# A decoder layer's attention scores recast as float32r products of high and low parts

## What is computed

```python
scores = jnp.einsum('bqhd,bkhd->bhqk', q, k) / sqrt(16)       # self
attn = jax.nn.softmax(scores, axis=-1)
...
scores = jnp.einsum('bhqd,bhkd->bhqk', q, k) / sqrt(16)       # cross
scores = jnp.where(mask == 0, jnp.float32(-1000000000.0), scores)
attn = jax.nn.softmax(scores, axis=-1)
```

## Time and profile before

| what | us |
|---|---|
| median of 3 runs | 2195.06 (2192.9 to 2195.93) |
| the profiled execution: its span, first to last instruction | 2190.0 |
| PE busy | 2124.8 |
| DVE busy | 1197.9 |
| ACT busy | 991.8 |
| POOL busy | 652.9 |

### The profile page before, as it was taken

How to read it: one execution, slowest core, us unless ns; L and a number is a source line. 1 busy time by engine, 2 the same in 40 slices (tenths; PEclk the granted TensorE clock), 3 DMA queues, 4 the chain that set the end, 5 groups by cost and what they waited for, 6 DMA issues and landing times. The chain is left out here.

```text
span 2190.0 us, 48112 instructions
## 1 busy us (share of the span) xinstructions
PE 2124.8 (97%) x18818; PEld 1490.5 (68%) x18818; DVE 1197.9 (55%) x2512; ACT 991.8 (45%) x1514; POOL 652.9 (30%) x1011
## 2 busy tenths in 40 slices
PE   8999999999999999999999999998799999999996
PEld 4566666666666666666666666665567877778785
DVE  4657667767667777667767766765311111111146
ACT  2445555555555555555555555555322222222233
POOL 2212332333332333332323332332421212122244
PEclk8999999999999999999999999999799999999998
DMA  3331112111111001101000100000023224331363
GB/s 98 100 104 50 36 42 74 34 50 57 34 33 33 28 27 34 32 24 29 24 24 31 33 26 27 24 25 16 21 59 80 50 53 90 80 75 30 85 214 154
DMA packets 96285, 116.98 MB, mean 53 GB/s; under 512 B 11360, under 2 KB 89005, under 8 KB 94016
## 3 DMA queue, kind: packets, MB, share of 16 engines
q1 hardware_dynamic: 66640, 82.37, 11.7%
q0 software_dynamic: 17184, 19.66, 5.0%
q10 hardware_dynamic: 12240, 11.88, 1.6%
HBM read 65.84 MB, written 56.05 MB: 56 GB/s over the span
## 5 line engine op out<-in xcount | busy, mean ns | idle before, releaser
L913 DVE TENSOR_REDUCE smax<-ps_s 128x4 f32<-128x1024 f32 x508 | 619.9, 1220 | 311.7 <-PE ps_s L614 277.2
L798 ACT ACTIVATE prob<-ps_e 128x1024 f32<-128x1024 f32 x508 | 519.7, 1023 | 499.9 <-PE ps_e L623 407.8
L614 PE MATMUL ps_s<-stack 17*128 17x256 f32 x4064 | 581.0, 403 | 20.1 <-DVE smax L913 13.6
L623 PE MATMUL ps_e<-stack 18*128 18x256 f32 x4064 | 580.1, 403 | 0.5 <-ACT prob L798 0.5
L614 PEld LDWEIGHTS ps_s<-stack 17*128 17x128 f32 x4064 | 353.4, 186 | 201.3 <-issue 103.6
L623 PEld LDWEIGHTS ps_e<-stack 18*128 18x128 f32 x4064 | 350.0, 186 | 1.5 <-DMA stack<-nrows 0.7
L1706 ACT ACTIVATE hid<-m_ps_h,b_sb 128x320 f32<-128x320 f32 x256 | 134.6, 527 | 392.3 <-PE m_ps_h L1660 392.3
L1660 PE MATMUL m_ps_h<-m_cols,w_sb 128*128 128x320 f32 x1024 | 290.8, 433 | 0.6 <-DVE m_cols L1729 0.6
L1677 PE MATMUL m_ps_o<-w_sb,hid 128*128 128x256 f32 x1280 | 279.2, 380 | 1.3 <-DVE m_res L1758 1.3
L1677 PEld LDWEIGHTS m_ps_o<-w_sb,hid 128*128 128x128 f32 x1280 | 243.8, 190 | 35.8 <-DVE m_res L1758 1.7
L639 PE MATMUL ps_w<-prob,val 128*32 128x256 f32 x4096 | 250.5, 386 | 1.2 <-ACT prob L798 1.2
(11 more groups left out here) (145 smaller groups left out, 2233.3 us busy)
## 6 DMA issues: line engine op xcount, KB each, us to landing
w_sb<-in_w SPq DMA_DIRECT2D x16, 1024.0 KB, 6.4
slot_rows_dram<-w_sb ACTq DMA_DIRECT2D x40, 258.0 KB, 2.6
m_rows<-slot_rows_dram SPq DMA_DIRECT2D x15, 645.0 KB, 4.4
xT<-in_xT SPq DMA_DIRECT2D x32, 256.0 KB, 2.9
ctxT<-in_ctxT SPq DMA_DIRECT2D x32, 256.0 KB, 2.9
x_res<-in_x SPq DMA_DIRECT2D x32, 256.0 KB, 2.8
sums_dram<-x SPq DMA_DIRECT2D x32, 256.0 KB, 2.1
c_rows<-sums_dram SPq DMA_DIRECT2D x8, 1024.0 KB, 15.9
```

Of the source, the lines that this page charges most:

```text
L614: mm = nc.tensor.matmul(scores[:, p % 2, t, :], rows_of_s[rows, Q, p // HG, t * P:(t + 1) * P], rows_of_s[rows, K, p // HG, :], start=True ...
L623: mm = nc.tensor.matmul(shifted[:, p % 2, t, :], rows_of_e[rows, K, h // HG, t * P:(t + 1) * P], rows_of_e[rows, Q, h // HG, :], start=Tru ...
L798: nc.scalar.activation(prob[:, h:h + 2, :].rearrange("p h s -> p (h s)"), shifted[:, :, :, :].rearrange("p h t s -> p (h t s)"), ACT.Exp, ...
L913: nc.vector.tensor_reduce(max_columns(X, p), scores[:, :, :, :], AX.X, ALU.max)\
```

## The change

Queries and keys are split into a high part that float32r holds exactly and the remainder, so that products of parts can be made in float32r matmuls that add up in PSUM.

- `padded` loses its mask and maximum rows. A strip of 32 now holds for keys the 16 features twice, for queries the 16 high and the 16 low parts. `stack` becomes three float32r tiles: `stack_q` (high and low queries), `stack_kh` (ACT's rounding copy of the keys) and `stack_kl` (the remainder, by DVE's new `key_remainders`, PSUM minus `stack_kh`). 
- A score is `stack_q` times `stack_kh` plus `stack_q` times `stack_kl`, 32 rows each. Mask and maxima stand in separate tiles `aux_q`, `aux_self`, `aux_cross`, and enter by a third product: of 4 rows for every shifted score, of 2 rows for CROSS scores. A duo has 24 matmuls with s CROSS and 20 with s SELF, where it had 8.
- DVE splits the maxima of each half into two parts (`split_maxima`, two instructions of 128x16), the transpose has 32 columns instead of 16, and `place_maxima` issues two DMAs instead of one. The mask is brought to rows once (`masks_by_row`, `store_masks`) and loaded by two DMAs for each CROSS item (`load_mask`).
- POOL makes the query parts: `query_parts` is a rounding copy and a subtraction, each of 128x512, behind `scatter` for CROSS and inside `turned_parts` for SELF, where the sum of the queries is also an instruction of its own. The keys' instructions write 512 elements a partition where they wrote 256 (CROSS). The two copies of the mask row (L1167) go.
- `STACK_Q` for SELF moves from behind duo 6 to behind duo 7.
- `w1_sb` of the second expert gets its memory only after attention and is loaded in the third turn of the experts' loop on SP. The constants set at the start change with the tiles.

```diff
@@ duo
-                for t in range(T2):
-                    if s is not None:
-                        for p in (2 * m, 2 * m + 1):
-                            rows = strip(p, SCORE_ROWS)
-                            mm = nc.tensor.matmul(scores[:, p % 2, t, :],
-                                                  rows_of_s[rows, Q, p // HG, t * P:(t + 1) * P],
-                                                  rows_of_s[rows, K, p // HG, :], start=True, stop=True)
...
+                def shifted_score(p, t, part):
+
+                    h = shifted_head(p)
+                    rows, at_side, g, out = strip(h, STRIP), side(e), h // HG, shifted[:, p % 2, t, :]
+                    if part == AUX:
+                        rows = strip(h, AUX_ROWS)
+                        keys_of = aux_self[rows, :] if Y == SELF else aux_cross[rows, bY % MASK_TILES, :]
+                        return nc.tensor.matmul(out, keys_of[:, t * P:(t + 1) * P], aux_q[at_side][rows, g, :],
+                                                start=True, stop=False)
+                    return nc.tensor.matmul(out, (stack_kh, stack_kl)[part][at_side][rows, g, t * P:(t + 1) * P],
+                                            stack_q[at_side][rows, g, :], start=False, stop=(part == LOW))
+
+                e_steps = [(t, part) for t in range(T2) for part in (AUX, HIGH, LOW)]
+                s_steps = e_steps if is_of(CROSS, s) else [(t, part) for t in range(T2) for part in (HIGH, LOW)]
+                for k in range(len(e_steps)):
...
@@ DVE
+            def key_remainders(Y, b, half):
+
+                dve.wait_ge(tr_ev[Y].sem, tr_ev[Y].count(b, 2 * half + 1))
+                groups = slice(2 * half, 2 * half + 2)
+                nc.vector.tensor_tensor(stack_kl[side((Y, b))][:, groups, :],
+                                        work("stack_k", Y, half).rearrange("p (g s) -> p g s", g=2),
+                                        stack_kh[side((Y, b))][:, groups, :].bitcast(F32), ALU.subtract)\
+                  .then_inc(low_ev[Y].sem, 1)
...
@@ POOL
+            def query_parts(Y, b):
+
+                if Y == CROSS:
+                    pool.wait_ge(qk_ev[CROSS].sem, qk_ev[CROSS].count(b))
+                else:
+                    pool.wait_ge(pad[SELF].sem, pad[SELF].count(b, 3))
+                ready()
+                whole = queries[Y].rearrange("p t (h r) -> p t h r", r=R)
+                high, low = (padded[Y][:, :, Q, :, part * R:(part + 1) * R] for part in (HIGH, LOW))
+                nc.gpsimd.tensor_copy(high.bitcast(F32R), whole).then_inc(pad[Y].sem, 1)
+                pool.wait_ge(pad[Y].sem, pad[Y].count(b, 4))
+                ready()
+                nc.gpsimd.tensor_tensor(low, whole, high, ALU.subtract).then_inc(pad[Y].sem, 1)
...
@@ emit of POOL
                 if is_of(CROSS, settled) and settled[1] < NB - 3:
                     scatter(settled[1])
+                if is_of(CROSS, n):
+                    query_parts(*n)
                 if is_of(SELF, n):
                     turned_parts(n[1])
@@ make_stack
-                if Y == CROSS and part == Q:
-                    pe.wait_ge(qk_ev[CROSS].sem, qk_ev[CROSS].count(b))
-                else:
-                    pe.wait_ge(pad[Y].sem, pad[Y].count(b))
+                pe.wait_ge(pad[Y].sem, pad[Y].count(b, keys_padded[Y] if part == K else None))
```

More of the change, by code:

```diff
@@ L25 @@
 BF16 = mybir.dt.bfloat16
+F32R = mybir.dt.float32r
 U32 = mybir.dt.uint32
@@ L259, in attend @@
         qk_ev = both("qk_ev", 6, 2)
-        pad = both("pad", 2, 5)
+        pad = both("pad", 5, 5)
         tr_mm = both("tr_mm", 4)
@@ L600, in duo @@
                     if m % 4 == 0:
+                        pe.wait_ge(low_ev[X].sem, low_ev[X].count(bX, m // 4 + 1))
                         pe.wait_ge(tr_ev[X].sem, tr_ev[X].count(bX, m // 2 + 2))
-                    scores, rows_of_s = score_tile(s, e, m), stack[side(s)]
+                    if m == 0 and X == CROSS:
+                        pe.wait_ge(mask_in.sem, mask_in.count(bX))
+                    scores = score_tile(s, e, m)
                     take_tile(scores, s_max[X], bX, m)
@@ L626, in duo @@
-                        if t == T2 - 1:
-                            mm.then_inc(e_mm[Y].sem, 1)
+                            mm = shifted_score(p, *e_steps[k])
+                        if k == len(e_steps) - 1:
+                            mm.then_inc(e_mm[Y].sem, 1)
+                    if s is not None and k < len(s_steps):
+                        for p in (2 * m, 2 * m + 1):
+                            mm = score(p, *s_steps[k])
+                        if k == len(s_steps) - 1:
+                            mm.then_inc(s_mm[X].sem, 1)
@@ L786, in stack_columns @@
                     act.wait_ge(e_mm[other[0]].sem, e_mm[other[0]].count(other[1], 4 * half + 4))
-                nc.scalar.copy(stack[side((Y, b))][:, part, 2 * half:2 * half + 2, :],
+                nc.scalar.copy((stack_q, stack_kh)[part == K][side((Y, b))][:, 2 * half:2 * half + 2, :],
                                work(name, Y, half).rearrange("p (g s) -> p g s", g=2)).then_inc(tr_ev[Y].sem, 1)
@@ L813, in max_rows, with masks_by_row @@
                     act.wait_ge(max_in[X].sem, max_in[X].count(b - 1))
-                nc.scalar.copy(nrows[X][half][:, :], work("max_rows", X, half)[0:H, 0:P]).then_inc(neg_ev[X].sem, 1)
+                nc.scalar.copy(nrows[X][half][:, :], work("max_rows", X, half)[0:PARTS * H, 0:P]).then_inc(neg_ev[X].sem, 1)
+            def masks_by_row():
+                act.wait_ge(masks_mm.sem, masks_mm.count(0))
+                nc.scalar.copy(mask_rows[:, :], work("masks", CROSS)[:, 0:P]).then_inc(masks_ev.sem, 1)
             def columns(X, b):
@@ L1095, in emit @@
                         maxima(*s, k, score_tile(s, e, k // 2))
+                    if s is not None and k in (H // 2 - 1, H - 1):
+                        split_maxima(*s, k // (H // 2))
+                    if s is not None and k == 5:
+                        key_remainders(*s, 1)
+                    if n is not None and k == 2 * slot_of(STACK_K, LATE_STACK_K, n) + 3:
+                        key_remainders(*n, 0)
                     if h == 0 and k == 3:
@@ L1136, in _ @@
             turn(0, 1)
+            key_remainders(SELF, 0, 0)
             half_steps(emit, dve)
```

192 lines of the change are left out of this document (125 added, 67 removed).

## The result

The changed kernel takes 2309.3 us (median of 4 runs, 2308.35 to 2310.94) against 2193.98 us (2191.46 to 2195.93) for the kernel before in the same session: 1.0527 times as long, 95% interval 1.0506 to 1.0548. Forecast were 2320 us, range 2230 to 2420, and slower with 0.90. The profiled execution took 2308.35 us, with a span of 2306.1, 116.1 longer than before.

What follows compares the result with a forecast made beforehand. PE's own chain was taken to bound attention. A turn 4.2 - 2.3 + 0.7 + 2.5 = +5.1 us, times 27 = +138; other duos -16, start +3: span 2190 to 2315, plus 5 is 2320 us, range 2230 to 2420.

Steps and rivals of the forecast that it cites:

- The duo: PE's group of score matmuls: 6 steps of 0.115 us plus 0.21 at its ends, 0.90 us instead of 1.08.
- rival of slow strips: Loads don't hide or float32r is no faster on PE: steps of 0.22 us, duo 1.53, total 2597; chance 0.08.
- The queries: CROSS queries, made on POOL behind the scatter, come late: PE stalls 4.8 us, the stretch grows 4.2 us a turn.
- A + 13.4: Forecast time of the queries, in us after A, the start of PE's products with values behind the fifth duo.
- The saved 13 duos: The turn's other 13 duos on PE save 0.18 us each, 2.3 us a turn.
- The clock: PE's clock falls to the lower level behind each stall: 2.5 us a turn, bounds 0 and 4.5.
- the prediction's two readings: Cost of low clock behind PE idleness: 1.7 us from the second idle stretch, 2.2 from the program's start.
- held-clock rival: The stalls are there, but PE keeps full clock behind them: 68 us less, 2252; chance 0.22.
- DVE: Added DVE work between two maxima makes PE wait: 0.7 us a turn, bounds 0 and 2.
- A turn: One turn of the pipeline, two half-steps with 16 duos: +5.1 us, times 27 turns = +138.
- the 88 other duos: Duos outside the 27 stalled turns save 0.18 us each, 16 us in all.
- faster: the queries come in time: POOL's indirect DMAs don't hold up the copy, queries ready before PE asks: turn 2.2 us shorter, 2123; chance 0.08.

Runs made afterwards that it cites:

- experiment 2: Changed kernel with 15 bf16 matmuls on PE ahead of its wait for the CROSS queries, in the 27 stalled turns: 2265.88 us.
- E1: Changed kernel with the query parts of a CROSS item ahead of the scatter's four indirect DMAs on POOL instead of behind them: 2168.99 us.
- experiment 3: E1 without DVE's key remainders, the low part of the keys set to zero once at the start: 2159.38 us.
- experiment 7: E1 with DVE's choice of experts two duos later and POOL's sum of residual and bias behind the placing of rows: 2150.46 us, rerun 2148.7 us.
- experiment 6: E1 without the products with the keys' low parts, 4 steps a duo instead of 6: 2112.88 us.
- experiment 5: Here its run of the kernel before with three unused POOL additions of 128x512 behind each SELF item's keys and queries: 2215.77 us.

## Why the prediction was right

The direction and the place were right, and 2309 lies 11 us under the forecast of 2320. The sizes inside were less exact and partly cancel, so that the total came this near is in part luck.

- **The duo**: forecast 0.90 us with steps of 0.115; measured 0.91 with steps of 0.12. The loads hide, and the rival of slow strips (2597) is out. The Trainium skill's rule on loads in the same row group (TensorE: Matmul & The Clock Gate, Part 3, The mechanism), by which a step would be 0.22, is contradicted: loads start 0.12 apart, each during the matmul before it. The same section also names a background weight buffer, into which a load may be pulled ahead; that the prediction left out, and it fits the trace. Its other sentence (FP8 and Floating Point Precision, TensorE Precision Notes) gave an estimate of 0.108, and the measurement lies near it.
- **The queries**: forecast at A + 13.4 and a stall of 4.8 us; measured A + 12.4 and 3.5. The scatter's 4.9 us and the subtraction's 1.27 were right. The term that was mis-sized is the copy: 1.1 taken, 0.63 measured, nearer to the 4-element cast of the earlier trace rows than I chose. The keys' end, at A + 5.1, was 0.3 early, and of the two waits of 0.2 the one between the fourth DMA and the copy isn't there. PE came 0.2 late. A turn's stretch grew by 3.2 instead of 4.2.
- **The saved 13 duos**: 2.3 forecast, 13 x 0.17 = 2.2 measured.
- **The clock**: 2.5 a turn forecast, 1.5 by experiment 2. The fall was right, the way back was faster: the level 0.50 ends some 0.9 us before the values' projection does. The lower of the prediction's two readings, 1.7, was the nearer one; I had leaned towards the startup, where the low level lasted longer. The held-clock rival is out by the windows and by experiment 2; but the measured total lies between it and my forecast.
- **DVE**: 0.7 a turn forecast; about 1.7 are left over, as the rest of 4.16 - 3.2 + 2.2 - 1.5, within the bounds of 0 and 2 but far from the value taken. It is the term that was furthest off. The reading under it was too low as well: 55% is DVE's share of the whole span. From 400 to 1500 us it was busy for 762.3 of the 1100 us before, 32.6 us a turn and not 26, and in E1 for 896.5, 37.6 us of a turn of 46.2. The forecast priced each DVE instruction by itself, and counted the remainders (0.3 by experiment 3) but not that POOL's added instructions stretch DVE's small ones. E1, free of stall and clock, gives the same rest on its own: 2.7 - 0.88 = 1.8.
- **A turn**: +5.1 forecast, +4.16 measured: 27 stalled turns 112 us instead of 138.
- **The first turns, the start and the end**: the 88 other duos were to save 16 us; the turns ahead of the first scatter save 4.3, start included. The first duo comes at 18.41 instead of 15.60, +2.8 (forecast 3). The end of attention costs 12.4, of which a stalled turn is 4.2; nothing of the rest was forecast. One piece is a wait new there: PE's timeline of the changed kernel at the end,

```profile
1594.78 0.38 PE L672 MATMUL ps_e<-aux_q,aux_cross 4*128 4x256 f32 x2 [3.24 <-DVE stack_kl L1008]
```

where with few duos left the remainders are not ready in time; just ahead of them on DVE a `split_maxima` of 1.26 us ends. Another is the 30th wait for L1277, 2.71 us at 1624.40, once more behind a scatter, with the clock at 0.50 behind it. The sum for the span was 2190 + 125 = 2315, and 2306.1 came: 26 too many in the turns (138 - 112), and 17 too few outside them (-13 forecast, 116.3 - 112.4 = +3.9 measured). The last 2 or 3 of the 11 us lie between span and time. The forecast took 5 from the median and a profiled execution of its own. In every run that lists both, the time is 1.8 to 2.3 us above the span, so most of the 5 was scatter between runs. A slip besides: 0.06 us in 439 duos widen the range by 26, not by 24.

- **The rival "faster: the queries come in time"** said 2123; E1 is the kernel in which they do, and takes 2169. By its own working a turn would be 2.2 shorter; 0.88 were. It has the same hole as the forecast: DVE's 0.7.

Open: of the 1.8 us a turn that E1 doesn't gain, the remainders are 0.3 (experiment 3) and the two moves of experiment 7 another 0.6, with `pick` still stretched. Roughly 0.9 are not traced to a place. The record narrows it down in one way. Before the first choice of experts, at 201.8 us in E1, a turn takes 45.02 us there and 47.01 in the kernel before, 2.0 less; from then on it takes about 46.1, while the kernel before stays at 47.0. So some 1.1 us come only when the choice of experts and the placing of rows are in the turn. That all of it is DVE's chain is suggested by the waits for `smax` and by experiment 6, and not shown.

## What to carry to other kernels

When work moves to an engine with a fixed order, find what it is put behind, long DMA issues above all: a cheaper product on the bounding engine is worth nothing while its operand waits, and one moved call was worth 140 us here. Charge an idle stretch of PE for the lower clock behind it too, here 1.5 us behind 3.5. And once PE's part shrinks, reckon the second engine as it runs beside the third, since a small DVE instruction can last until the POOL addition it meets has ended.

## What the hardware showed that was not expected

- Small DVE instructions with two inputs in SBUF are stretched by POOL's two-input instructions of 128x512 from 0.17 or 0.19 us to between 1.0 and 1.3, ending with them. In experiment 5 this held for one with a single input too: `base`, 128x4, took 1.01 us beside POOL's additions, a mean of 679 ns in that run.
- POOL's rounding copy of 128x512 from float32 to float32r takes 0.61 to 0.63 us, half of the two-input instruction of the same size (1.26).
- A float32r matmul of 256 columns advances a group of strips in 0.12 us, loads hidden, near the 0.108 that bf16's rate would give for as many columns.
- Behind 3.5 us of idleness PE's granted clock was at 0.50 from about 1049.0 to 1052.4, a shorter time than at the program's start. In experiment 6 it also fell to 0.50 in five of 26 turns, near 420 us with no wait longer than 0.43 us in the 12 us before, and those turns took 1.4 to 2.1 us more.
